# q's feature on ScalarE and GpSimd instead of VectorE in an attention and feed-forward block

## What is computed

```python
qkv = jnp.einsum('btc,ec->bte', x, Wqkv) + bqkv
q, k, v = jnp.split(qkv, 3, axis=-1)
q = jax.nn.elu(q * scale) + 1.0          # and k likewise
kv_cumsum, k_cumsum = jnp.cumsum(k * v, axis=1), jnp.cumsum(k, axis=1)
denom = jnp.clip(jnp.einsum('bthd,bthd->bth', q, k_cumsum), 1e-3, None)[..., None]
x = _layernorm(x + einsum(q * kv_cumsum / denom, Wproj) + bproj)
h = gelu(lowprec_linear(x, w_fc, b_fc))
out = _layernorm(x + lowprec_linear(h, w_proj, b_proj))
```

## Time and profile before

| | us |
|---|---|
| median of 3 runs | 276.52 (276.45 to 277.63) |
| profiled execution, first to last instruction (span) | 273.3 |
| VectorE busy | 238.9 |
| TensorE busy | 240.0 |
| GpSimd busy | 155.0 |
| ScalarE busy | 151.0 |

### The profile page before, as it was taken

How to read it: one execution, slowest core, us unless ns; L and a number is a source line. 1 busy time by engine, 2 the same in 40 slices (tenths; PEclk the granted TensorE clock), 3 DMA queues, 4 the chain that set the end, 5 groups by cost and what they waited for, 6 DMA issues and landing times.

```text
span 273.3 us, 3668 instructions
## 1 busy us (share of the span) xinstructions
PE 240.0 (88%) x1204; PEld 143.4 (52%) x1204; DVE 238.9 (87%) x513; ACT 151.0 (55%) x246; POOL 155.0 (57%) x118
## 2 busy tenths in 40 slices
PE   7999889997999899989999899989999989838761
PEld 7546636653566446644656356644664455524340
DVE  1398997998998999899989999899989997978962
ACT  2663277745556851855475754685285646332823
POOL 1076466575376656476566737675647656655851
PEclk9999999999999999999999999999999997979997
DMA  6940020036202473227304490238224530642022
GB/s 155 365 97 2 0 78 1 2 70 155 46 0 38 77 193 42 38 39 190 81 0 77 114 160 0 41 64 205 38 36 44 110 83 0 65 90 78 0 79 77
DMA packets 49474, 20.70 MB, mean 76 GB/s; under 512 B 38960, under 2 KB 49200, under 8 KB 49456
## 3 DMA queue, kind: packets, MB, share of 16 engines
q1 hardware_dynamic: 47824, 20.20, 32.7%
q10 hardware_dynamic: 1632, 0.27, 0.6%
HBM read 7.35 MB, written 4.19 MB: 42 GB/s over the span
## 4 chain that ended last, share of the span: by engine, by line
DVE 56%; PE 25%; DMA 8%; POOL 4%; issue 3%; ACT 2%; SPq 1%; ACTq 0%; POOLq 0%; DVEq 0%
DVE vbank L857 12%; PE abank L1116 8%; DVE hq L758 7%; DVE vbank L821 6%; PE dbank L1193 5%; DVE kvsum L799 4%; DMA h<-in_L_ffn_w_fc_dram 4%; POOL h_round L380 3%; PE hbank L1184 3%; DVE r L815 3%; DVE r L869 3%; DVE vbank L834 3%; DMA xqT<-xq 2%; DVE h_pow L750 2%; DVE kf L782 2%
## 5 line engine op out<-in xcount | busy, mean ns | idle before, releaser
L1116 PE MATMUL abank<-xT,WqkvT 128*128 128x512 f32 x176 | 81.6, 599 | 3.6 <-DVE kf L782 2.2
L380 POOL TENSOR_TENSOR h_round<-h,h_inv 128x1024 f16<-128x1024 f32 x32 | 66.5, 2079 | 31.2 <-DVE h_inv L753 28.5
L527 ACT ACTIVATE h<-hbank 128x512 f32<-128x512 f32 x64 | 36.7, 595 | 51.3 <-PE hbank L1184 51.0
L1116 PEld LDWEIGHTS abank<-xT,WqkvT 128*128 128x128 f32 x176 | 31.1, 190 | 36.2 <-issue 23.7
L857 DVE TENSOR_REDUCE vbank<-h 128x32 f32<-128x1024 f32 x32 | 39.1, 1221 | 1.6 <-ACT h L527 1.5
L349 POOL TENSOR_TENSOR qk<-qf,ksum 128x512 f32<-128x512 f32 x16 | 23.5, 1469 | 29.4 <-DVE ksum L794 18.6
L1184 PE MATMUL hbank<-w_fcT,xqT 128*128 128x512 bf16 x128 | 39.1, 387 | 0.0
L521 ACT ACTIVATE expz<-abank,zbias_neg 128x512 f32<-128x512 f32 x30 | 20.6, 687 | 31.9 <-PE abank L1116 31.4
L1193 PE MATMUL dbank<-w_prT,hT 128*128 128x256 bf16 x256 | 34.4, 279 | 1.9 <-DMA hT<-hq 1.3
L1148 PE MATMUL bbank<-WprojT,y 128*128 128x256 f32 x128 | 32.0, 380 | 0.0
L1193 PEld LDWEIGHTS dbank<-w_prT,hT 128*128 128x128 bf16 x256 | 25.2, 100 | 9.5 <-issue 3.3
(11 more groups left out here) (102 smaller groups left out, 357.4 us busy)
## 6 DMA issues: line engine op xcount, KB each, us to landing
x_sb<-in_L_attn_x_dram SPq DMA_DIRECT2D x8, 512.0 KB, 3.9
out_dram<-o_sb SPq DMA_DIRECT2D x7, 512.0 KB, 3.5
h<-in_L_ffn_w_fc_dram SPq DMA_DIRECT2D x1, 1024.0 KB, 9.6
h<-in_L_ffn_w_proj_dram SPq DMA_DIRECT2D x1, 1024.0 KB, 11.1
Wqkv_sb<-in_L_attn_Wqkv_dram SPq DMA_DIRECT2D x3, 256.0 KB, 6.3
out_dram<-o_sb SPq DMA_DIRECT2D x4, 128.0 KB, 1.7
hT<-hq SPq DMA_TRANSPOSE x28, 3.1
Wproj_sb<-in_L_attn_Wproj_dram ACTq DMA_DIRECT2D x1, 256.0 KB, 7.2
```

The lines of the kernel that those rows point to most:

```text
L380: nc.gpsimd.tensor_tensor(h_round[:, t % 2].rearrange("p (g j) -> p g j", j=BLOCK_K), h[:, t].rearrange("p (g j) -> p g j", j=BLOCK_K), h_ ...
L527: nc.scalar.activation(h[:, t, half * HALF:(half + 1) * HALF], hbank[half][:, :], ACT.Gelu).then_inc(s_h, 1)
L1116: last = nc.tensor.matmul(ps[:, :], WqkvT[:, k, e * P:(e + 1) * P], xT[:, k], start=(k == 0), stop=(k == CC - 1))
```

## The change

q's feature is formed in another way: elu(z) + 1 = exp(min(z, 0)) + max(z, 0). ScalarE's `activate` goes over q's bank a third time and writes the positive part into `qf`; GpSimd adds `expz` to it in place, at the head of `q_times_ksum`. VectorE's `feature` is left for k alone. A new semaphore `s_qpos` counts the positive parts; TensorE, which had waited for q's feature before it wrote q's bank again, now waits for the positive part. The wait for the last use of `qf` (`s_num`) goes from VectorE to ScalarE.

The core of the diff, with `...` for the places of the same kind (16 calls of `feature` for q in all, in the start, the loop and the steps written out, and the waits of TensorE that go with them):

```diff
@@ GpSimd @@
             def q_times_ksum(n, b, c):
+                wait(pool, s_qpos, 2 * n + c + 1)
+                nc.gpsimd.tensor_tensor(qf[:, c], qf[:, c], expz[:, 0, c], ALU.add).then_inc(s_f[0], 1)
                 wait(pool, s_f[0], 2 * n + c + 1)
                 wait(pool, s_ksum, 2 * n + c + 1)
                 nc.gpsimd.tensor_tensor(qk[:, c], qf[:, c], ksum[:, b, c], ALU.mult).then_inc(s_qk, 1)
@@ ScalarE, activate @@
                 nc.scalar.activation(expz[:, a, c], expz[:, a, c], ACT.Exp, scale=-1.0).then_inc(s_z[a], 1)
+                if a == 0:
+                    wait(act, s_num, 2 * n + c - 1)
+                    nc.scalar.activation(qf[:, c], ps[:, :], ACT.Relu, bias=zbias[:, row:row + 1]).then_inc(s_qpos, 1)
@@ VectorE @@
             def feature(n, a, c, ps):
-                dst = (qf, kf)[a]
                 row = CC * a + c
                 wait(dve, s_z[a], 2 * n + c + 1)
-                if a == 0:
-                    wait(dve, s_num, 2 * n + c - 1)
-                nc.vector.scalar_tensor_tensor(dst[:, c], ps[:, :], zbias1[:, row:row + 1], expz[:, a, c], ALU.add, ALU.max).then_inc(s_f[a], 1)
+                nc.vector.scalar_tensor_tensor(kf[:, c], ps[:, :], zbias1[:, row:row + 1], expz[:, a, c], ALU.add, ALU.max).then_inc(s_f[a], 1)
...
                 sum_k(n, n % 2, 0)
-                feature(n, 0, 0, abank[1])
...
@@ TensorE @@
-                wait(pe, s_f[0], 2 * n + 1)
+                wait(pe, s_qpos, 2 * n + 1)
                 project(n, 1, 1, abank[1])
...
-                wait(pe, s_f[0], 2 * n)
+                wait(pe, s_qpos, 2 * n)
                 transpose_x(n, n % 2, 0, abank[0])
```

More of the change, by code:

```diff
@@ L200, in block_kernel @@
         s_f = [sem(f"{a}_feature_ready") for a in "qk"]
+        s_qpos = sem("q_positive_part_ready")
         s_kv = sem("kv_ready")
@@ L888, in _ @@
             sum_k(0, 0, 0)
-            feature(0, 0, 0, hbank[0])
             feature(0, 1, 1, abank[1])
             sum_k(0, 0, 1)
-            feature(0, 0, 1, hbank[1])
             multiply_kv(0, 0, bbank[1])
@@ L906, in _ @@
             sum_k(1, 1, 0)
-            feature(1, 0, 0, abank[1])
             quantise_w(1)
@@ L913, in _ @@
             quantise_x(0)
-            feature(1, 0, 1, abank[0])
             sum_kv(1, 1, 0)
@@ L952, in step @@
                 n = s + 2
-                feature(n, 0, 1, abank[0])
                 n = s
@@ L992, in _ @@
             sum_k(6, 0, 0)
-            feature(6, 0, 0, abank[1])
             quantise_h(4, 3)
@@ L1000, in _ @@
             quantise_x(5)
-            feature(6, 0, 1, abank[0])
             residual_2(4, 0, 2)
@@ L1023, in _ @@
             sum_k(7, 1, 0)
-            feature(7, 0, 0, abank[1])
             quantise_h(5, 3)
@@ L1031, in _ @@
             quantise_x(6)
-            feature(7, 0, 1, abank[0])
             residual_2(5, 1, 2)
@@ L1249, in _ @@
             project(1, 2, 0, abank[0])
-            pe.wait_ge(s_f[0], 3)
+            pe.wait_ge(s_qpos, 3)
             project(1, 1, 1, abank[1])
@@ L1259, in _ @@
             transpose_w_pr(1)
-            pe.wait_ge(s_f[0], 4)
+            pe.wait_ge(s_qpos, 4)
             transpose_x(2, 0, 0, abank[0])
@@ L1355, in _ @@
             project(6, 2, 0, abank[0])
-            pe.wait_ge(s_f[0], 13)
+            pe.wait_ge(s_qpos, 13)
             project(6, 1, 1, abank[1])
@@ L1363, in _ @@
             project(6, 2, 1, abank[1])
-            pe.wait_ge(s_f[0], 14)
+            pe.wait_ge(s_qpos, 14)
             transpose_x(7, 1, 0, abank[0])
@@ L1395, in _ @@
             project(7, 2, 0, abank[0])
-            pe.wait_ge(s_f[0], 15)
+            pe.wait_ge(s_qpos, 15)
             project(7, 1, 1, abank[1])
```

## The result

Beside a median of 276.82 us for the kernel before on the same chip (276.45 to 277.63, four runs), the changed kernel takes **285.12 us** (283.80 to 287.89, four runs). The ratio is 1.030, 95% interval 1.023 to 1.036. The prediction was 281.9 us, with a range of 278.2 to 287.0. The profiled execution of the changed kernel is its slowest, 287.89 us with a span of 286.1; before, the span was 273.3. So the two traces lie 12.8 us apart where the medians lie 8.3 apart, and part of what the trace shows belongs to this one execution.

A forecast was written before the change was run, and what follows sets the result against it. It took TensorE's waits to bound the steps, despite VectorE's 87% busy share, and GpSimd the start. Start 3.1, chunk 1 1.6 and steps 0.7 made 5.4 us on 276.5: 281.9 us, range 278.2 to 287.0.

The forecast's parts named there:

- The forecast's own bounds: Whole kernel: 4.3 to 6.75 us slower, 280.8 to 283.3 us; the forecast had a 53% chance.
- rival (c): Steps: GpSimd keeps hq out for addition and qk, 1.44 us in each of five steps, 288.4 us; 11%.
- its queue: Chunk 0: four GpSimd instructions in a row, one held up by the weights' hq, start den 3.1 us later.
- the bounds of 2.0 and 3.6: Chunk 0: limits in us on the start's cost; 2.0 if hq doesn't stop GpSimd.
- Chunk 1: Chunk 1: hq holds up GpSimd's shift, 1.07 us, and part 1's denominators come 0.5 us later; 1.6 us.
- the upper bound of 2.3: Chunk 1: cost in us if part 1's addition also starts just ahead of xq and holds it up.
- The steps: Six steps: hq waits for GpSimd's addition, 0.17 us lost in each of four counted, 0.7 us in all.
- the open point of the working: Steps: whether hq waits for a GpSimd addition already running; 0.17 us lost if so, 0.10 gained if not.
- (b): Steps and chunk 1: VectorE's time comes back because TensorE doesn't hold kv and the residual; 270.6 us, 9%.
- (a): Start: only GpSimd's queue costs, neither hq in the steps nor shift is held up; +3.0 us, 279.5 us, 20%.
- (d): Start: its cost is hidden as den doesn't wait for the denominators, steps gain nothing; within 0.5%, 7%.

The follow-up runs named there:

- e4: The kernel before with chunk 0 alone in the new form of q's feature; 280.82 us, ratio 1.0105.
- e1: The kernel before with chunks 1 to 7 in the new form, chunk 0 old; 281.26 us, ratio 1.010.
- e11: The changed kernel with 30 transposes ahead of chunk 0's denominators, second weight's quantisation behind the k-v product, and 34 transposes in the tail; 276.64 us, ratio 0.9998.
- e7: The kernel before with chunks 2 to 7 in the new form and GpSimd's part 0 addition waiting for VectorE's hq; 278.07 us, ratio 1.001.
- e9: The kernel before with 34 unused identity transposes filling a TensorE pause in the tail; 274.71 us, ratio 0.994.
- e2: The kernel before with chunks 2 to 7 in the new form, chunks 0 and 1 old; 278.04 us, ratio 0.9996.
- e10: The changed kernel with 34 unused identity transposes filling a TensorE pause in the tail; 282.04 us, ratio 1.018.
- e3: The changed kernel with 20 unused identity transposes on TensorE ahead of chunk 0's denominators; 281.51 us, ratio 1.011.

## Why the prediction was right in sign and short in size

- **The number.** That 285.12 us lies in the range is partly luck. The forecast's own bounds ended at 283.3; the range went on to 287 for rival (c), a blocked hq that costs 1.44 us a step, and that is not what happened. The forecast was 5.4 us, measured are 8.3, and the difference is terms that the sum did not have.
- **The sign and the main cause.** Right: at the start GpSimd is the bound, and its queue costs. Predicted 3.1 us; measured 2.9 (e4), between the bounds of 2.0 and 3.6 (for 3.6 the prediction gives no working). The four instructions in a row, with the second addition held up by the weights' hq for 1.0 us, are there as written.
- **What lies behind the queue.** This is the term that was missing. The sum set the denominators at 1.92 us and the work behind them at its old length. But a queue of 3 us in front of TensorE is a pause of TensorE, 3.1 us in e4 and 3.69 in the changed kernel, and its granted clock fell to the 1.2 GHz level behind it. That cost 1.2 us in e4. In the profiled execution of the changed kernel it cost 1.6 in the denominators and 1.0 in the projection behind them (the first kvsum of chunk 1 comes 2.4 us later relative to the one ahead of it, of which e1 has 1.4 at full clock). The bounds of the start (up to 3.6) were bounds of the wait alone.
- **Chunk 1.** Right mechanism, 2.0 us instead of 1.6. The shift held up for a microsecond is 0.9 of it (e1 against e11). The rest is part 1, where the addition did start just ahead of xq and blocked it to 1.73 us: the case kept as the upper bound of 2.3.
- **The steps.** hq was blocked as forecast (1.31 us), which settles the open point of the working: VectorE's hq waits for the end of a GpSimd instruction that began ahead of it. The Trainium skill, SBUF — State Buffer, section "SBUF: two separate sides", has this as an exclusive lock for the whole instruction, and the trace agrees: 1.31 us beside the addition, 0.68 without it (e7). But the price was mis-sized, sign included. I had set hq's end at the addition's end plus a full hq, 0.17 late for kv; it ended 1.31 us after its start, and kv stands 2.08 us behind v's projection as before. An undisturbed step is 0.11 us shorter, not 0.17 longer. That TensorE holds kv and the third residual, so that 1.28 us of VectorE time come to almost nothing, was right: 0.61 us of idle time stand ahead of the third residual, predicted 0.6.
- **What hid that.** One late xqT (1.0 to 1.2 us) in the first steps, by coincidence with a transfer of instructions, brings the steps' sum to +0.3 us beside the trace of before and +1.0 beside that of e9. The predicted 0.7 lies between them, but it is right by luck: it was the sum of another effect.
- **The tail.** Not in the sum. It costs 2.2 us in the profiled executions and 1.7 in the mean of all ten traces with the pause left open, again by the clock behind a pause of TensorE; the times can't size it.
- **The sum.** The queue 2.9, the clock behind it 1.2 to 2.6, chunk 1 2.0, the steps 0.3 to 1.0 and the tail 1.7 make 8.1 to 10.2 us; measured are 8.3 (6.5 to 10.0 by the ratio). The 12.8 us between the two profiled executions are, by the marks, the late w_fc 1.3, the queue 2.9, the clock behind it 2.6, chunk 1 2.0, a further dip of the clock with a wait for hT in the first step 1.6, the steps behind it 0.1, and the tail 2.2. The late w_fc, which of the other traces only e11 has (1.0), and the 1.6, which none has, belong to that execution.
- **The rivals.** (b), VectorE's time comes back, was tested by e2: it does not, save 0.11 us a step. (c) would have shown as an hq kept out for two GpSimd instructions; it waited for one. (a) failed at the shift, (d) at den.

## What to carry to other kernels

Moving a pass off the engine with the most busy time brings what the next wait behind it allows: here 0.11 of 1.28 us a step, because TensorE's matmuls ended last at both places. And a delay in front of TensorE can cost more than its length: ask in the sum what the pause does to the granted clock and, for pauses as long as the ones here (3.1 us and more), price the next microseconds of matmuls at half speed; a few useless transposes in the pause (34 in 3.9 us) can buy that back, in the kernel before too.

## What the runs showed of the hardware that I had not expected

- Every pause of TensorE of 3.1 to 4.9 us (14 in the traces, in chunk 0 and in the tail) has a stretch at 1.2 GHz of 3.4 to 10.2 us, which begins between 1.4 us ahead of the pause's end and 2.0 us behind it. The Trainium skill, TensorE: Matmul & The Clock Gate, Part 1, says that the clock is gated down when TensorE has been idle; the traces agree, and keeping it busy through the pause kept it at 1.00 (e10, e11). Not every case is so plain: a remaining pause of 1.11 us was followed by 3.4 us at the low clock in e3, one of 1.08 us by none in e10, and in the kernel before the clock is low from 225.9 to 229.3 us with no pause longer than 0.7 us in the 8 us ahead.
- The lock between VectorE and GpSimd works in all directions seen: GpSimd's addition 2.24 us beside a VectorE hq, a 128x4 GpSimd shift 1.19 instead of 0.20, VectorE's hq 1.31 instead of 0.68 and xq 1.73. The blocked VectorE instructions end 0.55 us behind the addition, sooner than a full one would (hq 0.68).
- A DMA transpose of 1056 packets that lands after 3.0 us landed after up to 4.7 when a 16 KB transfer of instructions fell into it.
